# Four small moves in a one-core RWKV and mixture-of-experts kernel: known tokens' slots, gather indices, first parameters, halves of W2

## The reference, cut to what matters

```python
# mixer: per token r, w, k, v, kk, a from x and the token before it; 16 heads of 16 channels
s = s * w[:, :, None, :] + sa[..., None] * b[:, :, None, :] + v[..., None] * k[:, :, None, :]
y = einsum('bhij,bhj->bhi', s, q)          # 512 steps in a row, then group norm, gate, Wo
x = layernorm(x + mixer(x))                # these are the "rows" of x1
# experts: 8 experts, one per token, 256 -> 1024 -> 256
assign = argmax(x @ centroids.T)
h = relu(norm_e(x) @ W1[e] + b1[e]);  y = x + h @ W2[e] + b2[e]
out = layernorm(x + y)
```

## Time and profile before

| | |
|---|---|
| Median of 3 runs | 1126.01 us |
| The profiled execution | 1132.21 us, its span 1130.2 us |
| Busy: TensorE, VectorE, GpSimd, ScalarE | 1002.5, 789.9, 680.8, 547.7 us |
| DMA | 111.99 MB, 99 GB/s on average |
| The block loop ends, the experts' loop begins | about 791 us, about 805 us |

### The profile page before, as it was taken

One profiled execution on the slowest core, in us unless ns is written; L12 is line 12 of the kernel. 1 busy time (PEld: TensorE's weight loads), 2 busy tenths in 40 slices (PEclk: granted clock), 3 DMA queues, 4 the chain that ended last, 5 costly groups with the idle time before them and its releaser, 6 DMA issues.

```text
span 1130.2 us, 42039 instructions
## 1 busy us (share of the span) xinstructions
PE 1002.5 (89%) x16550; PEld 817.9 (72%) x16551; DVE 789.9 (70%) x1777; ACT 547.7 (48%) x1120; POOL 680.8 (60%) x1138
## 2 busy tenths in 40 slices
PE   4777999999999999999999998766299999999995
PEld 2546777777777777767867777653289898898894
DVE  3576797877879888768978887161566666666663
ACT  4464685665757766656856866221022222222221
POOL 1077988986888888878879889830123233233321
PEclk9678899988989999989999999585599999999998
DMA  4014033242242242241341341328744454554430
GB/s 100 12 37 82 16 87 87 32 95 52 57 105 56 53 105 54 55 105 30 79 97 30 87 96 24 84 58 277 289 152 166 173 181 150 174 178 146 172 126 4
DMA packets 208622, 111.99 MB, mean 99 GB/s; under 512 B 172364, under 2 KB 191952, under 8 KB 208080
## 3 DMA queue, kind: packets, MB, share of 16 engines
q1 hardware_dynamic: 204720, 101.31, 33.3%
q0 software_dynamic: 3744, 8.40, 2.2%
HBM read 85.42 MB, written 26.08 MB: 99 GB/s over the span
## 4 chain that ended last, share of the span: by engine, by line
PE 76%; DMA 7%; DVE 7%; issue 5%; ACT 2%; SPq 2%; POOL 0%; DVEq 0%; ACTq 0%; POOLq 0%
PE bank L551 20%; PE bank L866 12%; PE bank L879 8%; PE bank L633 6%; PE bank L686 6%; PE bank L641 5%; PE ry L879 4%; PE bank L596 4%; PE ry L714 2%; PE ry L663 2%; DMA scr_n<-arena 2%; PE bank L703 2%; DMA arena<-scr_n 2%; DVE arena L1378 1%; PE bank L584 1%
## 5 line engine op out<-in xcount | busy, mean ns | idle before, releaser
L1787 POOL TENSOR_TENSOR arena<-arena 128x30 f32<-128x30 f32 (+14 forms) x480 | 293.7, 612 | 36.4
L551 PE MATMUL bank<-arena 128*128 128x256 f32 (+2 forms) x992 | 294.2, 438 | 23.5 <-DVE arena L1262 10.1
L1790 POOL TENSOR_TENSOR arena<-arena 128x30 f32<-128x30 f32 (+14 forms) x480 | 285.8, 595 | 37.6
L551 PEld LDWEIGHTS bank<-arena 128*128 128x128 f32 x992 | 188.5, 214 | 79.9 <-issue 37.6
L866 PEld LDWEIGHTS bank<-arena 128*128 128x128 f32 x1248 | 147.5, 194 | 4.5 <-DVE arena L1686 2.6
L866 PE MATMUL bank<-arena 128*128 128x128 f32 x1248 | 148.1, 278 | 2.0 <-DVE arena L1686 2.0
L1378 DVE TENSOR_TENSOR arena<-bank,arena 128x512 f32<-128x512 f32 x128 | 79.4, 682 | 40.9 <-PE bank L633 40.6
L1192 ACT ACTIVATE arena<-arena 128x1 f32<-128x1 f32 x39 | 11.5, 295 | 177.6 <-DVE arena L1650 177.6
L879 PE MATMUL bank<-arena 128*128 x416 | 96.4, 385 | 0.1
L1818 POOL COPY arena<-arena 128x1 int32 (+1 forms) x39 | 7.1, 181 | 146.2 <-DVE arena L1714 146.2
L641 PE MATMUL bank<-arena 128*128 128x128 f32 x576 | 89.7, 296 | 5.3 <-DVE arena L1439 3.3
(11 more groups left out here) (167 smaller groups left out, 1672.2 us busy)
## 6 DMA issues: line engine op xcount, KB each, us to landing
arena<-in_W SPq DMA_DIRECT2D x47, 1024.0 KB, 5.0
scr_n<-arena SPq DMA_DIRECT2D x64, 128.0 KB, 2.8
arena<-scr_n SPq DMA_DIRECT2D x16, 512.0 KB, 4.6
scr_u<-arena SPq DMA_DIRECT2D x16, 512.0 KB, 2.9
arena<-scr_u SPq DMA_DIRECT2D x64, 128.0 KB, 2.9
arena<-in_xTp SPq DMA_DIRECT2D x32, 132.0 KB, 4.0
arena<-in_x SPq DMA_DIRECT2D x64, 64.0 KB, 2.1
scr_x<-arena SPq DMA_DIRECT2D x64, 64.0 KB, 2.9
```

Source lines behind the costliest of these rows:

```text
L551: mm = pe.matmul(ring.tile(m, name)[0:rows, to], lhsT, rhs, start=(i == 0), stop=(i == len(terms) - 1))
L1787: inv_ok.inc(f"m{s}", TT(t, U[:, 0:s, s:s + 1].broadcast_to(shape), U[:, s:s + 1, s + 1:TB].broadcast_to(shape), ALU.mult))
L1790: inv_ok.inc(f"a{s}", TT(U[:, 0:s, s + 1:TB], U[:, 0:s, s + 1:TB], t, ALU.add))
```

## The change

Four edits.

1. *Slots.* place_known and all seven mark_slots are moved in VectorE's body 16 to a place behind `tokens(14)`.
2. *Gathers.* The first three gathers take their indices from the table itself, with no copy.
3. *Start.* par, maa1T and maa2 are issued by ScalarE with a semaphore of their own (`first_in`), followed by a preload of the sigmoid table set. The engines wait for these and for the first eight constants; bonus_sum is made by VectorE after the first mixing stage, and who needs masks, mats or bonus_sum waits there. ScalarE leaves out its four table loads of body -2.
4. *W2.* The loads of experts 0 to 3 are issued after SP's body 15, those of experts 4 to 7 where all eight were.

```diff
@@ block.sync
-            early = [(par, d["par"]), (w_maa1, ...), (w_maa2, d["maa2"]),
-                     (masks, d["masks"]), (mats, ...)]
+            early = [(masks, d["masks"]), (mats, d["mats"].rearrange("m p n -> p m n"))]
...
-            def load_experts():
+            def load_experts(experts):
                 ring.wait_full(sp, last, "sc03", "sc13", "bk00", "bk01", "bk10", "bk11", "v0", "v1", "tg", "k", "r", "v")
                 comb.wait(sp, last, "u", "ao", "bm1", "km1", "q", "wend")
-                for e in range(E):
+                for e in experts:
                     sp.dma_start(W2[:, e], ...).then_inc(w2_in[e], 16)
...
             for n in BODIES:
                 body(n)
                 if n + 1 == last:
                     load_routing()
+                if n == last:
+                    load_experts(range(E // 2))
                 if n - 1 == last:
                     load_tokens(last)
-                    load_experts()
+                    load_experts(range(E // 2, E))
@@ block.tensor
             def weights(m):
                 if m == 0:
+                    pe.wait_ge(early_in, 32)
                     pe.wait_ge(w_in, 16 * d["_nloads"])
...
             def bonus(m):
+                if m == 0:
+                    pe.wait_ge(const_ok, 10)
...
-            pe.wait_ge(early_in, 80)
-            pe.wait_ge(const_ok, 10)
+            pe.wait_ge(first_in, 48)
+            pe.wait_ge(const_ok, 8)
@@ block.scalar
+            for dst, src in ((par, d["par"]), (w_maa1, ...), (w_maa2, d["maa2"])):
+                act.dma_start(dst, src).then_inc(first_in, 16)
+            nc.scalar.preload_act_table_set("sigmoid_and_others")
...
-                if n < last:                     # at each of the four table loads of a body
+                if -2 < n < last:
...
             def mask_v(m):
                 if m:
                     ring.wait_full(act, m - 1, "v0", "v1")
+                else:
+                    act.wait_ge(early_in, 32)
@@ block.vector
-            dve.wait_ge(early_in, 80)
-            for h in range(HALF):
-                nc.vector.tensor_scalar(bonus_sum[:, h, :], ...).then_inc(const_ok, 1)
-            dve.wait_ge(const_ok, 10)
+            dve.wait_ge(const_ok, 8)
+            dve.wait_ge(first_in, 48)
+            def bonus_weights():
+                dve.wait_ge(early_in, 32)
+                for h in range(HALF):
+                    nc.vector.tensor_scalar(bonus_sum[:, h, :], ...).then_inc(const_ok, 1)
...
-                if n == last + 1:
-                    place_known()
-                    mark_slots(0, 3)
                 if has(n - 1):
                     keep_x_odd(n - 1, 1)
-                if n == last + 1:
-                    mark_slots(3, 6)
...
                     mix_stage(n + 2)
+                if n == BODIES[0]:
+                    bonus_weights()
...
                 if has(n - 2):
                     tokens(n - 2)
                 if n == last + 1:
-                    mark_slots(6, 7)
+                    place_known()
+                    mark_slots(0, KNOWN // GROUP)
@@ block.gpsimd
             def gather(j, s):
-                if not (isinstance(j, int) and j < DEPTH):
+                if isinstance(j, int) and j < DEPTH:
+                    index = table[:, j:j + 1]
+                else:
                     prep.wait(w, j - DEPTH, "zb")
-                idx_ok.inc("gather", nc.gpsimd.tensor_copy(gidx[:, s:s + 1], table[:, bass.ds(j, 1)]))
-                idx_ok.wait(w, j, "gather")
+                    index = gidx[:, s:s + 1]
+                    idx_ok.inc("gather", nc.gpsimd.tensor_copy(index, table[:, bass.ds(j, 1)]))
+                    idx_ok.wait(w, j - DEPTH, "gather")
```

More of the change, by code:

```diff
@@ L319, in build @@
         w_in = sem("weights_in")
+        first_in = sem("first_in")
         early_in = sem("early_in")
@@ L409, in _ @@
             w = Waits(sp, carrier)
-            early = [(par, d["par"]), (w_maa1, d["maa1T"].rearrange("(k p) n -> p k n", p=P)), (w_maa2, d["maa2"]),
-                     (masks, d["masks"]), (mats, d["mats"].rearrange("m p n -> p m n"))]
+            early = [(masks, d["masks"]), (mats, d["mats"].rearrange("m p n -> p m n"))]
             loads = [(w_hid, d["hidT"].rearrange("(k p) n -> p k n", p=P)), (w_out, d["out2"].rearrange("w p n -> p w n"))]
@@ L909, in _ @@
             A = nc.scalar.activation
+            for dst, src in ((par, d["par"]), (w_maa1, d["maa1T"].rearrange("(k p) n -> p k n", p=P)), (w_maa2, d["maa2"])):
+                act.dma_start(dst, src).then_inc(first_in, 16)
+            nc.scalar.preload_act_table_set("sigmoid_and_others")
             half = lambda h: slice(h * COLS, (h + 1) * COLS)
@@ L1137, in body @@
                     keep_mk(n + 1)
-                if n < last:
+                if -2 < n < last:
                     log_exp_tables()
@@ L1180, in body @@
                     deviation(n - 1)
-            act.wait_ge(early_in, 80)
-            act.wait_ge(const_ok, 10)
+            act.wait_ge(first_in, 48)
+            act.wait_ge(const_ok, 8)
             for n in BODIES:
@@ L1247, in _ @@
             nc.vector.memset(within.rearrange("p (g t) -> p g t", t=TB)[:, :, 0:1], 0.0).then_inc(const_ok, 1)
-            dve.wait_ge(early_in, 80)
-            for h in range(HALF):
-                nc.vector.tensor_scalar(bonus_sum[:, h, :], head_sum, prm("faaaa", h), None, ALU.mult).then_inc(const_ok, 1)
-            dve.wait_ge(const_ok, 10)
+            dve.wait_ge(const_ok, 8)
[3 more added lines that the diff above has]
+                for h in range(HALF):
+                    nc.vector.tensor_scalar(bonus_sum[:, h, :], head_sum, prm("faaaa", h), None, ALU.mult).then_inc(const_ok, 1)
             def difference(m):
@@ L1807, in gather @@
             def gather(j, s):
-                if not (isinstance(j, int) and j < DEPTH):
+                if isinstance(j, int) and j < DEPTH:
+                    index = table[:, j:j + 1]
+                else:
                     prep.wait(w, j - DEPTH, "zb")
-                idx_ok.inc("gather", nc.gpsimd.tensor_copy(gidx[:, s:s + 1], table[:, bass.ds(j, 1)]))
-                idx_ok.wait(w, j, "gather")
+                    index = gidx[:, s:s + 1]
+                    idx_ok.inc("gather", nc.gpsimd.tensor_copy(index, table[:, bass.ds(j, 1)]))
+                    idx_ok.wait(w, j - DEPTH, "gather")
                 nc.gpsimd.indirect_dma_start(out=xg[:, s], out_offset=None, in_=x_rows,
-                                             in_offset=bass.IndirectOffsetOnAxis(ap=gidx[:, s:s + 1], axis=0),
+                                             in_offset=bass.IndirectOffsetOnAxis(ap=index, axis=0),
                                              bounds_check=NTOK - 1, oob_is_err=False).then_inc(gathered[s], 16)
```

## The result

| | median of 10 runs | lowest to highest |
|---|---|---|
| before | 1125.32 us | 1119.60 to 1127.64 |
| changed | 1134.20 us | 1126.22 to 1136.89 |

The account below looks back on a forecast made before the run. TensorE was taken to hold three quarters of the chain of waits, so edits matter only where it leaves TensorE. Terms -2.4 - 4.5 + 11.1 + 2.5 - 0.3 = +6.4 on the 1126.0 median gave 1132.4 us, range 1124.5 to 1136.5.

Parts of the forecast that it names:

- W2 in two parts: Loop's end: early W2 loads in SP's queue make block 15's inverse land 11.1 us later in DRAM.
- lower bound of 3.4: Inverse's store at the loop's end: only 3.4 us of delay, should the tokens not be held up either.
- Rival B: Inverse's store overtakes W2, leaving only the issue delay: 5.7 us in place of 11.1, sum +1.0; 20%.
- C: Four early W2 loads neither hold SP nor delay what follows; only gains remain, -7.2 us, 1118.8; 10%.
- Clock: Block 15's two solves: after TensorE's longer idling they run at 1.2 GHz, +2.5 us (bounds 0 and 2.9).
- Slots: Between last solve and read_out: known-token work leaves VectorE's path, 0.75 us in place of 5.24, -4.5.
- Start: Kernel start: ScalarE issues three small loads, VectorE's first difference comes at 5.9 instead of 8.3, -2.4 us.
- lower bound of 1.6: Kernel start: the gain should ScalarE's three transfers run in front of xT's bytes, 1.6 us.
- Rival D: TensorE stalls grow under W2's traffic or slots run into normed(15): +9 to +14; or read_out held otherwise, +10.9; 8%.
- Gathers: Before the first gather a copy and its wait go, -0.25 us; -0.3 taken, up to 3.4 more possible.

Follow-up runs that it names:

- e1: Changed kernel with the W2 edit undone, all eight loads issued where they were: 1120.5 us against 1126.4 for the kernel before, ratio 0.9989.
- e11: Repeat of the changed kernel with all eight W2 loads issued where they were: 1125.3 us against 1127.3 for the kernel before, ratio 0.9976.
- e3: Changed kernel with two W2 loads early in place of four, still issued by SP: 1127.2 us, ratio 1.0056 to the kernel before.
- e7: Changed kernel with two early W2 loads in place of four, issued by ScalarE instead of SP: 1124.8 us, ratio 0.9998 to the kernel before.
- e2: Kernel before with only the W2 edit, slots left in front of keep_x_odd: 1142.3 us, ratio 1.0183 to the kernel before.
- e6: Kernel before with only the slots edit: 1123.1 us against 1125.9, ratio 1.0006.
- e12: Kernel before with only the gathers edit: 1128.4 us against 1127.3, ratio 1.0021.
- e5: Changed kernel with the four early W2 loads moved directly behind the inverse's four loads: 1129.1 us against 1125.9 for the kernel before, ratio 1.0039.

## Why the prediction was right, step by step

- **W2 in two parts**, +11.1 forecast: the trip is 10.9 longer in the first trace, 11.4 in the second, and undoing the edit (e1, e11) takes the loss away. The store was issued 6.7 late, where 5.7 was forecast (the fourth load held SP 4.24, not 3.08). It landed 6.8 after its issue, where 8.1 was forecast. So the sum of the term is near by some luck, as a miss of +1.0 and one of -1.3 cancel; that the store lands with or after what SP issued ahead of it was right in the changed kernel and in e3. The place was wrong: I read it off SP's own stores behind SP's own loads, which can't tell one queue from shared engines; e7 does. TensorE idled 8.08 and 9.02 in front of the solves and not "over 10", for its own work ahead of them ended 10.1 after the inverse, where it had been 6.9. (The working's lower bound of 3.4 is 3.3 by its own numbers.) Rival B (only the issue delay) falls by e3, C (W2 hides) by all.
- **Clock**, +2.5: the solves took 7.04 against 4.35 and 4.63, so +2.7 and +2.4.
- **Slots**, -4.5: 0.86 in place of 5.24 and 4.12. The term is right in the sum but not in its owner: with early W2 the slots run inside the wait (e2), so it was W2 that brought it back, and the edit is worth its 3 to 4 only with W2 whole, by the traces of e6 and e1; their times do not show it.
- **Start**, -2.4: 1.4 between the first two traces, 1.9 between the means of the nine traces with the edit (6.3 to 7.0) and the five without (8.3 to 9.1). The term was too large since I let xT land as before. Its second half was issued at 1.5 and took 5.3, not 4.3; that ScalarE's 268 KB beside it is the reason is argued, not shown. The measured gain lies about at my lower bound of 1.6. ScalarE had three table loads ahead of its first tanh and two behind, not four ahead; nothing hangs on it.
- **read_out's own stall** was not in the sum: 2.53 us before, none in the three traces with four W2 loads ahead of the trip. That is -2.8 to keep_y, -2.2 by the second trace of before. (e12's trace, with W2 whole, has none either, so W2 is not the only way to lose it.) Why early W2 takes it away is open; the code packet in question started 3.0 ahead of read_out in the changed kernel and 0.9 behind its start before. Rival D had it the other way; it is what e5 shows, with W2 running beside the matmuls.
- **Gathers**, -0.3: the issue is 0.25 earlier; the landing depends on W1 and not on the copy.
- **Behind keep_y**: 27.4 or 29.4 to the table, in both kernels. In the changed kernel's first trace the clock stood at 1.00 in 775 to 778 (above), and the router's and gates' matmuls took 2.02.

The forecast sum of +6.4 stands beside 6.8 by the stretches and 8.9 by the medians. With the -2.8 of read_out's stall, which it left out, the sum would have been +3.6, and the interval (+7.7 to +14) leaves out even the +6.4. So the direction and the largest term are understood, but 1 to 3 us or more of the loss are not found in any stretch; they may lie in the loop, whose 13 us of spread would hide them.

## To carry to other kernels

Before moving a large load earlier, look for the small transfer that someone waits for, and price the wait at the landing of the bytes that any queue has issued by then, less what overtakes; here 4 MB cost a 512 KB round trip 11 us and won nothing: in the traces of before no wait for W2 was there to be saved. Edits that shorten one wait don't add: ask for each what it is worth once the others are in. And where the code outside the edit varies by 13 us between executions, cut the traces at fixed instructions and compare stretches.

## What the hardware showed that I had not expected

- Two 1 MB loads issued by ScalarE delayed the landing of a store issued by SP from 2.6 to 7.6 us (e7). With SP as issuer it was 6.3, the store itself issued 1.4 late (e3); the trip took 12.5 either way.
- TensorE's breaks without a visible wait grew from 0.2 to 0.9 up to 3.32 in the solves and from 1.7 to 2.5 up to 4.10 in read_out with 4 MB of loads beside them (e5), and each ends 2.2 to 3.1 after a packet of an instruction queue. In the changed kernel one of 3.74 stands at 740.91, hidden by the longer wait; that break took 3.5 to 4.6 in the five traces with W2 loads beside it and 1.3 to 1.8 in the nine others. In the three traces with four W2 loads ahead of the trip, TensorE having waited 7 to 9 us before the solves, the breaks in the solves and in read_out were gone.
- The order of a gather and three 1 MB loads within 2 us decides on 3 us of landing: 3.0 with the loads 1.64 behind, 3.5 at 1.12, 4.5 at 0.85, up to 6.6 with them ahead.
